# The first stage of an attention and expert layer: residual parts split from the PSUM banks, loads and weight products in another order

## The reference

```
qkv = x @ W_qkv.T + b_qkv                      # Q, K, V per head
attn = softmax(Q @ K.T / sqrt(8) + causal)
x = layernorm(x + (attn @ V) @ W_o.T + b_o)
q = x @ Wq; sim = q . keys                     # 4 heads x 2 halves x 64 keys
top 8 of each half, top 8 of their sums -> idx, scores
experts = sum over idx of silu(x . down[idx]) * softmax(scores) * up[idx]
mlp = silu(x @ Wg + bg) * (x @ Wu + bu) @ Wd + bd
out = layernorm(x + mlp + experts)
```

## Time and profile before

| | |
|---|---|
| runs | 824.59 us median of 3 (821.3 to 825.96) |
| profiled execution | 822.99 us, its span 821.3 us |
| PE busy | 714.6 us (87%) |
| DVE busy | 673.1 us (82%) |
| ACT busy | 567.6 us (69%) |
| POOL busy | 408.0 us (50%) |
| mean granted PE clock | 0.964 of full |

### The profile page before, as it was taken

How to read it: one execution, slowest core, us unless ns; L and a number is a source line. 1 busy time by engine, 2 the same in 40 slices (tenths; PEclk the granted TensorE clock), 3 DMA queues, 4 the chain that set the end, 5 groups by cost and what they waited for, 6 DMA issues and landing times. The chain is left out here.

```text
span 821.3 us, 17279 instructions
## 1 busy us (share of the span) xinstructions
PE 714.6 (87%) x4289; PEld 322.1 (39%) x4345; DVE 673.1 (82%) x2283; ACT 567.6 (69%) x922; POOL 408.0 (50%) x496
## 2 busy tenths in 40 slices
PE   6768999999999999999999997887989889788656
PEld 4422333332333333333333332333556456455345
DVE  5979999898998988998989995336987989879793
ACT  4720377666766766776667666669998988988871
POOL 8881122231122213212311222556999999999972
PEclk9975799999999999999999999998999999999997
DMA  6984536344533643463355315001001101100000
GB/s 181 287 204 115 117 74 143 92 91 110 131 82 76 140 114 75 100 142 88 90 112 132 83 38 132 28 17 54 2 1 39 39 1 40 40 0 14 2 12 27
DMA packets 58955, 67.06 MB, mean 82 GB/s; under 512 B 15488, under 2 KB 33536, under 8 KB 58880
## 3 DMA queue, kind: packets, MB, share of 16 engines
q1 hardware_dynamic: 53120, 62.35, 32.0%
q10 hardware_dynamic: 5184, 2.36, 1.0%
q0 software_dynamic: 576, 1.57, 0.7%
HBM read 46.73 MB, written 19.53 MB: 81 GB/s over the span
## 5 line engine op out<-in xcount | busy, mean ns | idle before, releaser
L805 ACT ACTIVATE probs<-ps 128x384 f32<-128x384 f32 (+2 forms) x384 | 292.3, 809 | 179.0 <-PE ps L870 177.0
L770 POOL TENSOR_SCALAR_AFFINE_SELECT probs<-probs 128x256 f32<-128x256 f32 x256 | 103.0, 407 | 359.1 <-ACT probs L805 356.7
L956 DVE CUSTOM_DVE_ANT_0 junk<-ps,tri 128x256 bf16<-128x256 f32 (+3 forms) x512 | 228.6, 487 | 21.6 <-PE ps L838 18.4
L838 PE MATMUL ps<-QK 128*128 128x512 bf16 (+3 forms) x735 | 222.5, 343 | 26.3 <-DVE mx L960 12.4
L870 PE MATMUL ps<-Qa,Ka 128*128 128x512 bf16 (+3 forms) x745 | 175.0, 328 | 8.0 <-issue 2.5
L960 DVE TENSOR_REDUCE mx<-ps 128x1 f32<-128x512 f32 x256 | 162.0, 681 | 17.8 <-issue 10.1
L856 PE MATMUL ps<-probs,Vg 128*9 128x512 f32 (+3 forms) x1536 | 154.0, 490 | 0.0
L838 PEld LDWEIGHTS ps<-QK 128*128 128x128 bf16 x768 | 69.4, 97 | 214.1 <-DVE mx L956 87.8
L1123 POOL TENSOR_TENSOR QK<-front 128x1024 f32<-128x1024 f32 x60 | 115.8, 1951 | 0.0
L1231 ACT ACTIVATE ps<-QK,nb 128x512 f32<-128x512 f32 x128 | 83.2, 682 | 16.1 <-DVE A L1403 14.3
L1403 DVE SCALAR_TENSOR_TENSOR A<-QK,rows,ps 128x511 f32<-128x511 f32 x128 | 89.8, 738 | 3.0 <-ACT ps L1231 2.6
(11 more groups left out here) (138 smaller groups left out, 828.4 us busy)
## 6 DMA issues: line engine op xcount, KB each, us to landing
QK<-q_scr SPq DMA_DIRECT2D x48, 192.0 KB
QK<-k_scr SPq DMA_DIRECT2D x48, 192.0 KB
Qa<-q_scr SPq DMA_DIRECT2D x48, 192.0 KB
Ka<-k_scr SPq DMA_DIRECT2D x48, 192.0 KB
o_scr<-Os SPq DMA_DIRECT2D x32, 256.0 KB, 2.1
q_scr<-front SPq DMA_DIRECT2D x34, 128.0 KB, 3.5
k_scr<-front SPq DMA_DIRECT2D x18, 128.0 KB, 4.2
xin<-in_L_attn_x_dram ACTq DMA_DIRECT2D x8, 256.0 KB, 4.4
```

What stands on the lines that cost most here:

```text
L770: pool.affine_select(out=diag, in_=diag, compare_op=ALU.is_ge, fill=0.0, base=0, pattern=[[0, 2], [1, P]], channel_multiplier=-1).then_inc ...
L805: act.activation(probs[:, k % 2, hh, 0:width], ps[:, bank:bank + 2, :].rearrange("p a c -> p (a c)")[:, 0:width], ACT.Exp, scale=SM_SCALE) ...
L838: pe.matmul(ps[:, X_BANK + f % X_SLOTS, 0:c1 - c0], Qx[:, u, hh, P * i:P * (i + 1)], Kx[:, u, hh, c0:c1], start=True, stop=True).then_inc( ...
L956: dve.tensor_tensor_reduce(out=junk[:, f % 4, 0:w], in0=src, in1=tri[:, CHUNK - w:CHUNK], scale=1.0, scalar=-BIG, op0=ALU.add, op1=ALU.max ...
```

## The change

- **Split.** ACT no longer writes `qf`. DVE computes `rf` in one instruction from the PSUM bank, the bias and part 0 (`scalar_tensor_tensor`: bank + bias - part 0). The cast of `rf` to part 1 is ACT's, at the end of its iteration, behind `r_made`; `xbT` moves behind the first parts. PE's projection of chunk n now also waits for the subtraction of n - 2, which reads the bank.
- **Start.** The four small loads have two semaphores: the weights alone (`wqkv_loaded`), and the three biases. `WqkvT` is transposed through bank 7, and PE waits for its copy only before the first projection. SP issues the loads of x chunks 0 and 1 as its first work. The first waits of DVE for the biases stand in `values`.
- **Order on SP.** The loads for the first maxima are issued behind chunk 3's stores, those of chunks 4 and 5 behind the loads.
- **Weights.** The 18 weight loads move to ACT's queue at the start of attention, their f32 buffers lie in `probs`, and `kbdT` is cleared by POOL there, behind `tri`. PE makes the weight products one by one between the 18 maxima ahead, and waits for all copies (`wT_read`, 6) behind them.

```diff
-                    for b in range(BATCH - 1):
-                        store_parts(sp, b)
+                    for u in range(2):
+                        sp.dma_start(xin[:, u, :, :], x_chunks[u]).then_inc(x_loaded[u], 16)
+
+                    for n in range(4):
+                        store_parts(sp, n)
...
                     load_parts(sp, Qx[:, 0], Kx[:, 0], bass.ds(0, 1), xop_loaded[0])
-                    sp.wait_ge(wts_loaded, 16 * 7)
+                    for n in range(4, 2 * BATCH - 2):
+                        store_parts(sp, n)
...
-                    turned_weights(1, 0, WqkvT[:, :, :])
-                    act.wait_ge(wqkv_loaded, 64)
+                    turned_weights(act, 1, 7, WqkvT[:, :, :])
+                    act.wait_ge(bias_loaded, 48)
...
-                            act.wait_ge(xT_read, n + 1 + FREE)
-                            act.activation(xbT[:, n, :], xT[:, u, :], ACT.Identity, bias=bo_col[:, 0:1]).then_inc(xb_made, 1)
                             if b > 1:
                                 act.wait_ge(qk_stored[n % QS], STORES * 16)
                             for w in range(2):
                                 act.wait_ge(qk_ready, 2 * n + w + 1)
-                                if b > 0:
-                                    act.wait_ge(r_made, 2 * (n - 2) + w + 1)
-                                act.activation(qf[:, u, w, :], ps[:, 2 + 2 * w + u, :], ACT.Identity,
-                                               bias=bqk[:, w:w + 1])
                                 act.activation(qs[:, n % QS, w, 0, :], ps[:, 2 + 2 * w + u, :], ACT.Identity,
                                                bias=bqk[:, w:w + 1]).then_inc(q_read, 1)
+                            act.wait_ge(xT_read, n + 1 + FREE)
+                            act.activation(xbT[:, n, :], xT[:, u, :], ACT.Identity, bias=bo_col[:, 0:1]).then_inc(xb_made, 1)
+                            for w in range(2):
+                                act.wait_ge(r_made, 2 * n + w + 1)
+                                act.activation(qs[:, n % QS, w, 1, :], rf[:, u, w, :], ACT.Copy).then_inc(p2_made, 1)
...
                             pe.wait_ge(q_read, 2 * n + w + 1)
+                            if b > 0:
+                                pe.wait_ge(r_made, 2 * (n - 2) + w + 1)
...
-                            dve.tensor_tensor(rf[:, u, w, :], qf[:, u, w, :], qs[:, n % QS, w, 0, :],
-                                              ALU.subtract).then_inc(r_made, 1)
-                            dve.wait_ge(r_made, 2 * n + w + 1)
-                            dve.tensor_copy(qs[:, n % QS, w, 1, :], rf[:, u, w, :]).then_inc(p2_made, 1)
+                            dve.scalar_tensor_tensor(out=rf[:, u, w, :], in0=ps[:, 2 + 2 * w + u, :],
+                                                     scalar=bqk[:, w:w + 1], in1=qs[:, n % QS, w, 0, :],
+                                                     op0=ALU.add, op1=ALU.subtract).then_inc(r_made, 1)
+                        values(b, u)
...
+                    def weight_product(n):
+
+                        if n == 0:
+                            pe.wait_ge(prep_loaded, 16 * 11)
+                            pe.matmul(ps[:, 0, 0:P], wo_nat, center[:], start=True, stop=True).then_inc(wT_ready, 1)
+                        elif n <= 3 * FC:
+                            bank, c = divmod(n - 1, FC)
+                            mm = pe.transpose(ps[:, 1 + bank, P * c:P * (c + 1)], (down_nat, wq_nat, kbdT)[bank][:, c, :],
+                                              ident[:])
+                            if c == FC - 1:
+                                mm.then_inc(wT_ready, 1)
+                        else:
+                            c = n - 1 - 3 * FC
+                            pe.wait_ge(wT_read, 5)
+                            mm = pe.matmul(ps[:, 0, P * c:P * (c + 1)], WqT[:, c, :], kbd[:, c, :], start=True, stop=True)
+                            if c == FC - 1:
+                                mm.then_inc(wT_ready, 1)
+
                     for f in range(CPG):
                         max_chunk(0, f, 0, LOADS * 16)
                     for f in range(AHEAD):
                         max_chunk(CPG, f, 1, LOADS * 16)
+                        if f < 4 * FC + 1:
+                            weight_product(f)
+                    pe.wait_ge(wT_read, 6)
```

More of the change, by code:

```diff
@@ L392, in build, with store_parts, turned_weights @@
         STORES = 6
[L394 to L402, removed]
+        def store_parts(sp, n):
+            b, u = divmod(n, 2)
+            sp.wait_ge(p2_made, 2 * n + 2)
+            slot = n % QS
+            for s in (0, 1, 3, 4):
+                sp.dma_start(q_part(b, u, s), qs[:, slot, 0, s % PARTS, :]).then_inc(qk_stored[slot], 16)
+            for s in (0, 1):
+                sp.dma_start(k_part(b, u, s), qs[:, slot, 1, s, :]).then_inc(qk_stored[slot], 16)
+        def turned_weights(act, n, bank, dst):
+            act.wait_ge(wT_ready, n)
+            src = ps[:, bank, 0:dst.free_size()]
+            if len(dst.shape) == 3:
+                src = src.rearrange("p (a b) -> p a b", b=P)
+            act.activation(dst, src, ACT.Copy).then_inc(wT_read, 1)
         with ExitStack() as phase:
@@ L646, in build @@
             probs = sa("probs", [P, 2, GH, 2 * CHUNK])
+            early = probs[:, 0, :, 0:CHUNK].rearrange("p h (c d) -> p h c d", d=P)
+            late = probs[:, 1, :, 0:CHUNK].rearrange("p h (c d) -> p h c d", d=P)
+            down_nat, wq_nat, kbdT, WqT = [early[:, k] for k in range(4)]
+            kbd, wo_nat = late[:, 0], late[:, 1, 0]
             Vg = sa("Vg", [P, 2, SEQ // P, GH, VW])
@@ L670, in _ @@
                     load_parts(sp, Qx[:, 1], Kx[:, 1], bass.ds(1, 1), xop_loaded[1])
[L672 removed]
+                    for n in range(2 * BATCH - 2, 2 * BATCH):
+                        store_parts(sp, n)
                     for u in range(2):
@@ L784, in _ @@
                     act.sem_inc(exp_done, FREE)
+                    act.dma_start(down_nat, down.rearrange("(c p) d -> p c d", p=P)).then_inc(prep_loaded, 16)
+                    act.dma_start(wq_nat, Wq.rearrange("p (c d) -> p c d", d=P)).then_inc(prep_loaded, 16)
+                    act.dma_start(wo_nat, W_o).then_inc(prep_loaded, 16)
+                    act.wait_ge(kbd_zeroed, 1)
+                    for p in range(2):
+                        for h in range(RH):
+                            hl = h % 2
+                            act.dma_start(kbdT[64 * hl:64 * hl + 64, 2 * p + h // 2, 64 * hl:64 * hl + 64],
+                                          keys[h, :, p, :]).then_inc(prep_loaded, 16)
+                    act.dma_start(Wg_sb[:], Wg).then_inc(wts_loaded, 16)
+                    act.dma_start(Wu_sb[:], Wu).then_inc(wts_loaded, 16)
+                    act.dma_start(Wd_sb[:], Wd.rearrange("(c p) d -> p c d", p=P)).then_inc(wts_loaded, 16)
+                    act.dma_start(up_sb[:], up.rearrange("(c p) d -> p c d", p=P)).then_inc(wts_loaded, 16)
+                    for i, bias in enumerate((bg, bu)):
+                        act.dma_start(bgu[:, i, :], bias.rearrange("(c p) -> p c", p=P),
+                                      allow_slow_non_contiguous=True).then_inc(wts_loaded, 16)
+                    act.dma_start(bd_col[:], bd.rearrange("(p o) -> p o", o=1),
+                                  allow_slow_non_contiguous=True).then_inc(wts_loaded, 16)
+                    for n, (bank, dst) in enumerate(((0, WoC[:, :]), (1, downT[:, :]), (2, WqT), (3, kbd),
+                                                     (0, Wsim[:, :, :]))):
+                        turned_weights(act, n + 2, bank, dst)
+                    act.wait_ge(wts_loaded, 16 * 7)
                     def copy_out(n, half):
```

86 lines of the change are left out of this document (20 added, 66 removed).

## The result

The changed kernel takes 810.64 us (median of 4, 810.05 to 812.24), the kernel before 823.48 in the same number of runs: a ratio of 0.985 [0.981, 0.988], 12.8 us less. In later series a few executions took 1.36 to 2.33 ms; the ratios leave them out, the medians keep them, which moves none by more than 0.2.

The account below looks back on a forecast made before the run. DVE was taken to bound the first stage, then the border, the QK loads and DVE again. Terms 3.6 + 3.4 + 3.3 - 1.0 = 9.3 us off 822.99 gave 813.7, put down as 814.5, range 811 to 820.

Parts of the forecast that it names:

- Start: Kernel start: PE's transposes wait for the weights alone and x loads go first, so P(0) comes at 6.5, 3.6 us earlier.
- Rest of the first stage: First stage behind P(0): x loads set a period of 4.2 us, the block ends at 41.5, gain 3.4.
- Loads: Border to the first maxima: loads issued from 28 are hidden, first reduction at 44.0, gain 3.3 us.
- Products: Weight products on PE between the 18 maxima ahead of the first scores: a loss taken as 1.0 us.
- Rival 2: Products at half clock: DVE starves between the maxima ahead; gain 6.8, time 817; chance 0.12.
- rival 3: First maxima's loads land late, held up by stores and x7; at 47, gain 6.2, time 817.5; chance 0.10.
- rival 1: First stage bound by engines, not x loads: block ends at 39.5, gain 11.3, time 812; chance 0.12.
- Rival 4: Slower x loads in the first stage: no gain left from 8.8 us a load; chance 0.10 together with rival 5.
- a start that comes earlier is handed on to the end: Attention groups: they pace themselves and no instruction looks at an absolute time, so an earlier start reaches the end.
- Rival 5: Behind the earlier start: a later wait takes the gain, at most all, 823; chance 0.10 together with rival 4.
- Or if the group stage changes its length: Attention groups: a changed length was one of the signs by which the prediction would be wrong; no size given.

Follow-up runs that it names:

- order back: Changed kernel with the loads for the first maxima put back behind chunk 5's stores: 815.95 us, 0.991 of the kernel before.
- twice the transposes: Changed kernel with each of the 12 transposes between the maxima made twice, same result: 811.64 us, 0.987 of the kernel before.
- 16 and 8 memsets: Changed kernel with two or one unread one-column DVE memsets added per first-stage chunk: 812.98 us with 16, 810.84 with 8.
- the two kernels above: Kernel before with only the first maxima's loads moved ahead of chunks 4 and 5's stores: 819.10 us; changed kernel with that move undone: 815.95.

## Why the prediction was right in direction and short in size

**Up to the first scores it held as a sum, 9.3 against 9.3, with terms that moved against each other.**

- *Start*, 3.6: 3.4. P(0) at 6.73 for 6.5; PE had x0 at 4.4 (4.5 forecast) and x1 at 5.8 (5.3).
- *Rest of the first stage*, 3.4: 3.1, the block's end at 41.97 for 41.5. The mechanism is the one forecast, PE waiting for xin and DVE idle ahead of its subtractions, and it was shown by issuing those loads earlier (P(7) 7 us earlier). P(4) came at 22.38 for 23.7, P(6) at 31.54 for 32.1, P(7) at 35.83 for 34.8. The forecast gave 2.7 from P(6) to P(7) and it took 4.29, with the clock at 0.50 from 31.95 to 35.36 behind the wait for chunk 7; where PE waited less for it (0.7 to 1.9) the clock stayed and the step was 2.61 (order back, twice the transposes, 16 and 8 memsets). The x loads took 3.8 at the median where I took 4.2, that of chunk 7 the full 5.2. ACT's cast took 0.62 for 0.7, the subtraction from the bank 0.75 for 0.72, POOL's 1.15 to 1.18 for 1.15. The x load went out 3.44 behind the projection (22.38 to 25.82) where I had 3.6.
- *Loads*, 3.3: 2.9 in the two timelines (3.1 to 3.6 by the two kernels above), and no wait for QK is left. But DVE reduced 2.9 behind the last subtraction instead of 2.5, 0.36 of it because POOL's last store had not landed, so the first reduction came at 44.84 for 44.0: 9.45 for 10.3.
- *Products*, 1.0: 0.15 (36.27 against 36.12; the kernel before again had 36.23). This is the term mis-sized here, and it makes up for the 0.85 by which the other three fell short together; that the sum came out at 9.3 is luck. I priced them at the lower clock; it was full for most of the stretch. Rival 2 is out, and rival 3 with it, since PE waited for no load at the border; rival 1 is out as the period averaged 4.16 (29.10 over 7 chunks), not the 3.8 of the engines, and PE waited for xin (its 812 is nearer to the measured time than 814.5, by luck). Rival 4 needed x loads of 8.8 or more, the longest was 5.2.
The Trainium skill (TensorE: Matmul & The Clock Gate, Part 4: PE-mode transpose) would have left the clock at half for longer, since by it transposes don't count as activity. The trace is against the loss worked out by that rule, 3.5: the clock rose in the stretch into which the transposes were put, and no later with twice as many. The runs don't say whether it was the transposes or the fuller mix of maxima and transposes (PE busy 2.82 of 3.00 us from 69 to 72; before, 9.91 of 11.00 from 79 to 90 in the earlier trace rows) that did it. Maxima alone can: in the kernel before the clock stood at 1.00 from 65.1 to 68.5, behind five us in which PE was busy 4.81, and fell again.

**Behind the first scores the prediction failed.** The step is "a start that comes earlier is handed on to the end": it was handed on, but I took the length of what follows as fixed. The group stage became 2.4 shorter, and 1.1 to 2.6 shorter in the profile of every kernel that has the split and no memsets. That is the cause of most of the miss. Against 814.5: 2.4 from the groups, 0.3 from the last stage, 0.8 since I set the forecast above the profile's 813.7 towards the median of three runs, and 0.4 by which the median of after lies below its profiled execution, 3.9 in all. Rival 5, which asked the right question of that stage, looked for a loss alone. "Or if the group stage changes its length" was the condition under which I called myself wrong, and it is what happened. The range was also cut close: its own gain of 12.5 on 822.99 leaves 810.5, which was put down as 811.

What the runs show of it, in two parts that need not have to do with each other.

- *The clock at the first scores.* From the first scores to the next group's transposed maxima it took 14.94 before and 14.29 after, 0.65 of the 2.4. Before, the clock reached 1.00 only 2.0 behind the first scores; after, 8 us ahead of them. The eight profiles with the products between the maxima have 14.28 to 14.29 there, the six without, in which the clock rises 0.8 to 2.1 behind the first scores, 14.46 to 15.01. So the products, priced at a loss of 1.0, cost 0.15 ahead of the first scores and gave 0.65 behind them, which the sum had at nothing.
- *The late start on DVE.* The floor of the even groups goes with the number of DVE instructions ahead of the loop, whatever else is changed, and 16 memsets bring the late start back (27.52) or take it from the kernel before (27.24). Seven groups at 0.26 make 1.8. In this pair of profiles the seven together are 0.9 shorter (193.7 and 192.8), because groups stand above their floor for other reasons too; over all profiles they average 194.7 with the late start and 192.9 without.

The remaining 0.9 lies in the odd groups (0.4) and behind the last maxima (0.5), where profiles with the same floor differ by as much, and is not explained. What is argued only: that the place of DVE's code matters, and not its number as such. -8, -16 and +16 give one floor and 0 the other, which a place would do and a count would not, but no run moved the code without adding to it. It stays open.

**The border.** From the last subtraction to the first instruction on POOL of the next block it took 1.33 before, 1.32 with the loads behind, 1.3 to 1.7 in the two profiles of the changed kernel, 2.1 with twice the transposes, 2.7 with earlier x loads, 2.9 with 16 memsets and 3.4 with 8. In all of these POOL's DRAIN ended either 1.07 to 1.08 behind the last subtraction or 0.54 to 0.55 behind the landing of POOL's last store, whichever is later, and the next block began 0.24 to 0.25 behind it. (In the split alone ACT's last copy was later still, and the border 1.82.) That store was issued at 34.4 to 34.5 in every kernel made from the changed one and landed at 41.3 to 42.9 with the loads for QK ahead, at 37.5 with them behind. The border is where about 1 of the 2.6 us went by which earlier x loads end the subtractions sooner. No run moved this store, and no version that I ran beats the changed kernel.

## What to carry to other kernels

When the unit that sets a stage's period is relieved, write down the next loop through all queues (here an x load, issued behind a subtraction, behind a bank read), and its period comes out to a few tenths; loads that stand at a border must be moved with it, since the split alone gained nothing at the first scores, and the loads' place 3.1 to 3.6 in either kernel. Work put between products at the lower clock need not cost what its durations there say: here the clock rose among it, and that paid in the stage behind. An engine's own last store can hold up the end of a block long after its last computation, so look when it lands. And leave room in the range for stages that are not edited: compare the length of a repeated group before and after, to a hundredth, before the gain or loss of a few us is put down to what was changed.

## What the runs showed of the hardware that I had not expected

- A repeated group's shortest length goes with how many instructions an engine has ahead of it: 27.51 us or 27.25, with a start 0.21 late behind a register instruction of the sequencer that is itself late, in seven of 16 groups. Sixteen instructions that do nothing brought it or took it away.
- Twelve f32 transposes of 128 columns, and twelve more, between 18 maxima cost 0.15 us and nothing, and the granted clock went from 0.50 to 1.00 in that stretch in all eight profiles. In the first stage, behind a wait of PE of 2.18 us, it fell to 0.50 at 31.95 and was back at 35.36.
- The border of two blocks took 1.3 to 3.4 us between the last and the first instruction of POOL, with the same code there: POOL's DRAIN ended 0.54 behind the landing of its last store, where that was what it waited for.
- POOL's last store of 128 KB took 3.1 us to land with the six loads for QK behind SP's stores and 6.9 to 8.4 with them ahead.
- Four issues of SP's stores took 4.77 us in the changed kernel (24.75 above) against 2.52 in the earlier trace rows.
